# Order of the four products of a gate and up tile: both gate products first, then both up products

## The reference, cut to what matters

```python
# x: (4, 512, 512), context: (4, 512, 256)
query, key = context @ Wq.T + bq, context @ Wk.T + bk
attention = softmax(query @ key.T)
x = x + layernorm(x) @ attention.T          # per batch
h = layernorm(x)
gate = h @ gate_w.T                         # gate_w, up_w: (2048, 512), cubic splines
up = h @ up_w.T                             # through some 8000 control points each
inter = silu(gate) * up                     # (4, 512, 2048)
out = x + inter @ down_w.T                  # down_w: (512, 2048), a spline too
```

## Time and profile before

| | |
|---|---|
| median of 3 runs | 286.06 us (284.72 to 287.19) |
| the profiled execution, its time | 285.89 us |
| its span in the trace | 283.9 us |
| PE busy | 263.8 us, 93% |
| DVE, POOL, ACT busy | 182.0, 132.9 and 125.2 us |
| gate and up tiles of batches 0 to 3 begin at | 71.2, 129.4, 187.6 and 245.6 us |

### The profile page before, as it was taken

How to read it: one execution, slowest core, us unless ns; L and a number is a source line. 1 busy time by engine, 2 the same in 40 slices (tenths; PEclk the granted TensorE clock), 3 DMA queues, 4 the chain that set the end, 5 groups by cost and what they waited for, 6 DMA issues and landing times.

```text
span 283.9 us, 3824 instructions
## 1 busy us (share of the span) xinstructions
PE 263.8 (93%) x1250; PEld 168.4 (59%) x1252; DVE 182.0 (64%) x322; ACT 125.2 (44%) x202; POOL 132.9 (47%) x138
## 2 busy tenths in 40 slices
PE   7699479997999999999999999999999999599995
PEld 3232167763654858865548588755375888364674
DVE  0699977887457774764567838646587476464403
ACT  3044623325767702257767222557674133353300
POOL 0489462579653811309718123078083131594800
PEclk9959959999999999999999999999999999999999
DMA  6899044000720000032600000226000001100003
GB/s 188 312 424 409 2 131 168 0 2 0 267 105 0 3 0 0 2 148 90 279 0 0 0 0 0 94 76 274 0 0 0 0 0 74 74 0 2 0 0 148
DMA packets 7209, 23.23 MB, mean 82 GB/s; under 512 B 1184, under 2 KB 2336, under 8 KB 5792
## 3 DMA queue, kind: packets, MB, share of 16 engines
q1 hardware_dynamic: 7200, 23.11, 21.7%
HBM read 18.92 MB, written 4.19 MB: 81 GB/s over the span
## 4 chain that ended last, share of the span: by engine, by line
PE 73%; DVE 13%; ACT 5%; issue 4%; DMA 2%; POOL 1%; SPq 1%; ACTq 0%; DVEq 0%; POOLq 0%
PE bank L1304 11%; PE bank L1350 10%; PE bank L1306 9%; PE bank L1324 7%; PE bank L1157 5%; PE bank L1254 5%; PE bank L1255 4%; PE bank L1256 4%; PE bank L1168 4%; PE bank L1357 3%; DVE prod L856 3%; PE bank L1211 3%; DMA power<-in_g_power 2%; DVE prob L840 2%; DVE inter L947 1%
## 5 line engine op out<-in xcount | busy, mean ns | idle before, releaser
L1107 POOL TENSOR_TENSOR ih<-inter,ones 128x512 fp32r<-128x512 f32 x64 | 65.7, 1042 | 35.2 <-DVE inter L947 33.7
L947 DVE TENSOR_TENSOR inter<-inter,bank 128x512 f32<-128x512 f32 x64 | 43.4, 687 | 26.0 <-ACT inter L762 26.0
L762 ACT ACTIVATE inter<-bank 128x512 f32<-128x512 f32 x64 | 37.7, 599 | 25.1 <-PE bank L1306 24.5
L733 ACT ACTIVATE qk<-bank,nmr,rstd 128x512 f32<-128x512 f32 x16 | 12.5, 780 | 46.7 <-PE bank L1256 46.7
L1350 PEld LDWEIGHTS bank<-d_r,ih 128*128 128x128 f32 x256 | 30.6, 192 | 4.1 <-issue 3.2
L1304 PE MATMUL bank<-xh,gate_r 128*128 128x512 f32 x64 | 29.9, 467 | 1.5 <-DVE zg L939 1.5
L1350 PE MATMUL bank<-d_r,ih 128*128 128x192 f32 x256 | 31.1, 274 | 0.0
L1324 PE MATMUL bank<-inter,d_u 128*64 128x512 f32 x128 | 30.1, 602 | 0.0
L1304 PE MATMUL bank<-xh,up_r 128*128 128x512 f32 x64 | 27.2, 425 | 1.4 <-DVE inter L947 1.3
L1091 POOL TENSOR_TENSOR xres<-x,ones 128x2048 f32<-128x2048 f32 x4 | 14.4, 3602 | 23.9 <-DMA out<-xres 23.6
L1306 PE MATMUL bank<-zg,gate_v 102*128 102x512 f32 x64 | 25.3, 395 | 0.0
(11 more groups left out here) (100 smaller groups left out, 458.2 us busy)
## 6 DMA issues: line engine op xcount, KB each, us to landing
x<-in_x SPq DMA_DIRECT2D x4, 1024.0 KB, 4.8
xT<-in_xT SPq DMA_DIRECT2D x4, 1024.0 KB, 6.9
out<-xres SPq DMA_DIRECT2D x16, 256.0 KB, 2.1
ctxT<-in_ctxT SPq DMA_DIRECT2D x4, 512.0 KB, 7.6
rd<-in_d_r SPq DMA_DIRECT2D x2, 768.0 KB, 6.4
knots<-in_d_knot SPq DMA_DIRECT2D x1, 1280.0 KB, 12.1
d_coef<-in_d_coef SPq DMA_DIRECT2D x1, 1024.0 KB, 14.8
d_pt<-in_d_node SPq DMA_DIRECT2D x1, 1024.0 KB, 16.9
```

Source lines behind the costliest of these rows:

```text
L762: nc.scalar.activation(inter[:, m], gbank[m % 2][:], ACT.Silu).then_inc(s["silu_done"], 1)
L947: V.tensor_tensor(inter[:, m], inter[:, m], ubank[m % 2][:], ALU.mult).then_inc(s["mult_done"], 1)
L1107: G.tensor_tensor(ih[:, m], inter[:, m], ones[:, 0].broadcast_to([P, TOK]), ALU.mult).then_inc(s["ih_done"], 1)
```

## The change

Before, the order in a tile is G1, U1, G2, U2. After, it is G1, G2, U1, U2. The waits stay with the products they stand with: `silu_done` ahead of G1, `mult_done` ahead of U1. Nothing is added and nothing is removed. The other engines' programs are the same.

```diff
-                    for n, (dst, read) in enumerate(((gbank, "silu_done"), (ubank, "mult_done"))):
+                    for n, (dst, read, done) in enumerate(((gbank, "silu_done", "g_mm"), (ubank, "mult_done", "u_mm"))):
                         if m >= 2:
                             pe.wait_ge(s[read], MT * b + m - 1)
                         mm(dst[m % 2][:], gu_r[n][:, a, w * P:(w + 1) * P], xn2r[:, a], start=True, stop=False)
-                    for n, (dst, done) in enumerate(((gbank, "g_mm"), (ubank, "u_mm"))):
                         mm(dst[m % 2][:], gu_v[n][:, i], zg[:], start=False, stop=True).then_inc(s[done], 1)
```

## The result

The new order takes 281.49 us (median of 4 runs, 281.06 to 281.77) against 286.61 before: a ratio of 0.9839, 95% interval 0.9807 to 0.9872. The profiled execution took 281.58 us with a span of 279.6, 4.3 us less than before. The forecast was 280.9, and the range 279.1 to 283.3.

What follows compares the result with a forecast made beforehand. TensorE's own queue was taken to bound the kernel, its waits between products being the gain. 3 x 1.12 (batches 0 to 2) + 1.67 (batch 3) = 5.0 us off 285.89 gave 280.9 us, range 279.1 to 283.3.

Steps and rivals of the forecast that it cites:

- What bounds: TensorE's queue sets the end; ahead of line 1304 it waits 36 times for VectorE's multiply, 11.9 us.
- The chain of 1.81 us and its seven or nine steps: G2(m) to U1(m+2) needs 1.81 us; seven old steps give 1.63, nine new ones 2.10, so undisturbed stretches keep no wait.
- Batch 3, 1.67: Gain in batch 3: 1.12 us in the ten tiles ahead of `down_basis`, 0.55 in tiles 10 to 15.
- Batches 0 to 2, 1.12 each: Gain per batch: 0.74 in tiles 0 to 7, 0.15 at the third energy product, 0.23 at tile 10.
- the 0.74 of tiles 0 to 7: Batches 0 to 2: first energy product 0.74 us earlier, with a wait left at tile 6.
- What it might cost, 0: Product steps in the new order: no lengthening expected, with 1.3 us kept on either side.
- Rival 4: A bank's second product waits for the first to drain: 21 us over its pairs, time 299; chance 0.04.
- Rival 3, U2: VectorE's multiply held by U2 instead of the activation, so the wait returns; up to 285.9, no gain; chance 0.04.
- my cover of 0.16: At VectorE's multiply: U2 would allow its start 0.91 us behind G2, ScalarE's result only 1.07.
- Rivals 1 and 2: Rival 1: middle batches' chain doesn't move, 282.8, chance 0.09. Rival 2: all waits go, 278.4, chance 0.04.
- rival 5: The Trainium skill page's short step of some 131 ns per product, giving 270 us; chance 0.01.
- Sum: Whole kernel: 3 x 1.12 + 1.67 = 5.0 us gained, from 285.89 to 280.9; chance 0.78.

Runs made afterwards that it cites:

- 3: Also spelled up_first: order U1, U2, G1, G2 in every tile, against the kernel before; 296.07 us, ratio 1.0357.
- 2: Old order everywhere, with a third up bank (bank 6) in batch 3, against the kernel before; 284.68 us, ratio 0.9931.
- 4: Also spelled even_tiles: new order on even tiles alone, old order on odd ones, against the kernel before; 286.77 us, ratio 1.002.
- 5: New order on even tiles alone plus ten filling products ahead of batch 3, against the kernel before; 284.34 us, ratio 0.9925.
- experiment 7: Also spelled new_split_qk: new order, ScalarE's key evacuation in batches 0 to 2 moved behind tile 5's activation; 281.72 us, ratio 0.9837 to the kernel before.
- experiments 1: New order in batch 3 alone, old order in batches 0 to 2, against the kernel before; 284.73 us, ratio 0.9933.
- old_split_qk: Old order with ScalarE's key evacuation moved behind tile 5's activation in batches 0 to 2, against the kernel before; 286.65 us, ratio 1.0028.
- new_again: The changed kernel run once more, unaltered, as a neighbour for later runs; 282.45 us, ratio 0.9875 to the kernel before.

## Why the prediction was right

The steps in its own order.

- *What bounds.* Right: TensorE's queue, and the waits of line 1304 in it. One remark on the clock row was wrong: the full clock does not begin behind the first 17 us, as the earlier trace rows itself shows a 5 in the sixth slice, 35 to 43 us. Nothing hung on it.
- *The chain of 1.81 us and its seven or nine steps.* Right, and shown, not only argued: five steps give a wait of 0.64 (3), an extra bank removes the wait in the old order (2), and a change of half the tiles moves the waits to the other half (4, 5).
- *Batch 3, 1.67.* Measured 1.65. GpSimd did not come into the way.
- *Batches 0 to 2, 1.12 each.* Measured 1.03. In batch 1, which the working was made for, the 0.74 of tiles 0 to 7 is exact (0.71 in batch 0), with the wait left at tile 6, and experiment 7 shows whose it is: ScalarE's double evacuation. Tile 10 gave its 0.24. At the third energy product 0.11 came instead of 0.15. The rest is about 0.05 us that tiles 11 to 15 take longer than before (147.18 to 153.64 against 148.91 to 155.32) and which I can't put to one cause.
- *What it might cost, 0.* Right: the mean step in the new order is the old one, and up_first, with pairs as well, has it too. Rival 4 is out.
- *Rival 3, U2.* Its mechanism exists, but only behind a U1 that has waited, at tile 6: VectorE starts 0.50 us behind U2, not 0.44, so my cover of 0.16 was 0.10. Elsewhere the activation is still the later one.
- *Rivals 1 and 2.* The chain of the middle batches did move, and not all waits went. The Trainium skill's step of 131 ns (rival 5) is in none of the gate and up products: where they wait for nothing they step by 0.2335 in both orders, as 129.76 to 129.99 between G1 and G2 in batch 1 after.
- *Sum.* 5.0 forecast, 4.74 in the stages and 4.87 with the clock kept. What the prediction left out is the clock in batch 3. I read the window of one execution of before, saw 1.00, and took it for a property of the kernel. In another execution of the changed kernel it cost 1.5 us, nearly as much as the whole gain of that batch. The sum has no term for it. A loss of the size of even_tiles', 22.96 - 20.51 = 2.45 us, would have put the time outside the range; that the runs met none or a smaller one is luck. The changed kernel was 281.49 us in one set of runs and 282.45 in another.

## What to carry to other kernels

With two buffers per output and two consumers in a row, count the steps between the product that releases the first consumer and the product that needs the second one's buffer. Putting the early consumer's products together lengthens that distance by two steps for nothing, one at either end, and in batch 3 it was worth a third buffer. Do it for all tiles: in half of them it only moved the wait there. And look at the granted clock where the tensor engine comes out of an idle stretch in several executions, not one, and compare stages as well as times, before a difference of a microsecond is put down to an edit.

## What the runs showed of the hardware that was not expected

Between the products with `g_basis` and tile 0 of batch 3 TensorE does 0.7 us of work in 3.7 us. Out of this same stretch it came at a granted clock of 1.00 in the profiled executions of before, of the changed kernel's first runs and of experiments 1 and 2. In those of even_tiles and up_first it came at 0.50 (1.2 GHz) and kept it for 6.1 us of the stage. In new_split_qk and old_split_qk it kept it for some 3 us, and in new_again the clock fell only 0.8 us after the products had begun again. The three executions with the shortest part ahead of tile 0 (70.28 to 70.45 us, with a mean clock of 0.93 there, against 0.90 or 0.91 in all the others) are three of these five. What decides it stayed open. Ten filling products in the stretch kept the clock at 1.00 in the profiled stages of all four kernels that had them. The Trainium skill, TensorE: Matmul & The Clock Gate, section Part 1: The HAM clock gate, has the clock halved by default and released by activity, and what watches the activity running free of the kernel's start. That agrees with two executions of one kernel differing here (18.85 and 20.37 us in batch 3), and no run here shows more of it than the rows above.
